# Cross-attention and feed-forward kernel: keys projected once instead of twice, their rotated half made by a DMA swap, context buffered twice

## The reference, cut to what matters

```python
# x: (4, 256, 128), ctx: (4, 512, 128); 16 heads of 64; B = 4 batches
lat = layer_norm(_layernorm(x), ln_lat_g, ln_lat_b)
ctx = layer_norm(context, ln_ctx_g, ln_ctx_b)
q = (lat @ Wq)                      # 256 x 1024 in each batch
k, v = split(ctx @ Wkv)             # 512 x 1024 each
# each head of 64 channels has two halves of 32
k = concat([k1 * cos - k2 * sin, k2 * cos + k1 * sin])
attn = softmax(clip(q k^T * 64 ** -0.5, -11, 11))
x = x + (attn v) @ Wo + bo
x = x + ffn(_layernorm(x))          # a second layer: products of 16 heads of 8, softmax,
                                    # two projections, 8 gated experts
```

## Time and profile before

| | |
|---|---|
| median of 3 runs | 391.61 us (391.37 to 391.96) |
| the profiled execution's own time | 388.52 us |
| its span, first to last instruction | 386.4 us |
| mean granted TensorE clock | 0.93 |
| TensorE matrix products busy | 321.9 us (83%) |
| VectorE busy | 269.6 us (70%) |
| GpSimd busy | 217.0 us (56%) |
| ScalarE busy | 155.5 us (40%) |

### The profile page before, as it was taken

One profiled execution on the slowest core, in us unless ns is written; L12 is line 12 of the kernel. 1 busy time (PEld: TensorE's weight loads), 2 busy tenths in 40 slices (PEclk: granted clock), 3 DMA queues, 4 the chain that ended last, 5 costly groups with the idle time before them and its releaser, 6 DMA issues.

```text
span 386.4 us, 6595 instructions
## 1 busy us (share of the span) xinstructions
PE 321.9 (83%) x2566; PEld 215.9 (56%) x2566; DVE 269.6 (70%) x459; ACT 155.5 (40%) x282; POOL 217.0 (56%) x200
## 2 busy tenths in 40 slices
PE   6699999999999989789999999599998986630444
PEld 6476666667776656457766566377665545310131
DVE  4886426337754799777585999774549879599844
ACT  3464544555324546215345556343444540100500
POOL 4767344355544483929346677973445876546070
PEclk9999999999999999969999999999999999755656
DMA  8730000000000000000000000000000000000000
GB/s 248 181 53 2 27 2 1 2 2 3 0 2 2 1 2 0 3 0 2 2 0 2 1 2 2 1 15 2 1 2 0 2 3 14 0 0 0 0 0 27
DMA packets 10157, 5.82 MB, mean 15 GB/s; under 512 B 2768, under 2 KB 9744, under 8 KB 10128
## 3 DMA queue, kind: packets, MB, share of 16 engines
q1 hardware_dynamic: 9072, 5.29, 5.3%
q10 hardware_dynamic: 1056, 0.13, 0.2%
HBM read 4.89 MB, written 0.52 MB: 14 GB/s over the span
## 4 chain that ended last, share of the span: by engine, by line
PE 53%; DVE 23%; POOL 10%; issue 6%; ACT 5%; DMA 2%; SPq 1%; DVEq 0%; POOLq 0%; ACTq 0%
PE sc L493 11%; PE pv L507 11%; PE sums L523 5%; POOL prod L823 5%; PE pj_k L434 5%; DVE prod L815 4%; PE pj_k L436 4%; PE pj_k L435 4%; DVE att L1003 4%; ACT e L688 3%; DVE o L1020 3%; PE side L580 3%; DMA prod<-in_L_xattn_Wq_dram 2%; DVE prod L823 2%; POOL wvS L1212 1%
## 5 line engine op out<-in xcount | busy, mean ns | idle before, releaser
L688 ACT ACTIVATE e<-sc 128x1024 f32<-128x1024 f32 x64 | 65.7, 1026 | 100.9 <-PE sc L493 100.9
L1225 POOL TENSOR_SCALAR e<-e 128x1024 f32<-128x1024 f32 x64 | 71.6, 1119 | 34.7 <-ACT e L688 30.9
L1218 POOL TENSOR_TENSOR krot<-kcos,ksin 128x512 f32<-128x512 f32 x32 | 41.7, 1304 | 69.7 <-DVE ksin L903 69.7
L493 PE MATMUL sc<-qs,ks 64*128 64x256 f32 x768 | 62.5, 295 | 6.3 <-ACT e L688 5.7
L493 PEld LDWEIGHTS sc<-qs,ks 64*128 64x128 f32 x768 | 49.4, 185 | 28.5 <-issue 16.6
L507 PE MATMUL pv<-e,v 128*64 128x256 f32 x512 | 64.0, 393 | 0.0
L507 PEld LDWEIGHTS pv<-e,v 128*64 128x64 f32 x512 | 34.5, 139 | 24.2 <-issue 9.3
L903 DVE TENSOR_TENSOR kcos<-pj_k,cosT 128x512 f32<-128x512 f32 x32 | 22.0, 688 | 30.2 <-PE pj_k L436 29.8
L523 PE MATMUL sums<-e,sum_rows 128*32 128x256 f32 x512 | 30.9, 382 | 5.3 <-POOL e L1225 5.3
L840 DVE TENSOR_TENSOR ks<-krot,ks 128x512 fp32r<-128x512 f32 x32 | 34.0, 1063 | 0.0
L823 POOL TENSOR_TENSOR prod<-att,kv 128x1024 f32<-128x1024 f32 x8 | 27.7, 3474 | 8.9 <-ACT att L779 8.6
(11 more groups left out here) (215 smaller groups left out, 596.3 us busy)
## 6 DMA issues: line engine op xcount, KB each, us to landing
ctx_in<-in_ctx_dram SPq DMA_DIRECT2D x4, 256.0 KB, 5.0
prod<-in_L_xattn_Wkv_dram SPq DMA_DIRECT2D x2, 512.0 KB, 6.0
x_in<-in_x_dram SPq DMA_DIRECT2D x1, 512.0 KB, 5.8
prod<-in_L_xattn_Wq_dram SPq DMA_DIRECT2D x1, 512.0 KB, 6.6
wo<-in_L_xattn_Wo_dram SPq DMA_DIRECT2D x1, 512.0 KB, 8.4
fwe<-in_L_ffn_We_dram SPq DMA_DIRECT2D x1, 512.0 KB, 4.3
out_dram<-x_in SPq DMA_DIRECT2D x4, 128.0 KB, 1.8
fbup_r<-in_L_ffn_bup_dram SPq DMA_DIRECT2D x1, 128.0 KB, 6.5
```

The costliest lines, as they stand in the source:

```text
L493: last = nc.tensor.matmul(sc[:, h, c * NT:(c + 1) * NT], ks[rows, j % 3, k_part, chunk], qs[rows, j % 2, q_part, :], start=(k_part + q_par ...
L688: nc.scalar.activation(e[:, j % 3, :, 2 * half:2 * half + 2, :].rearrange("p h c n -> p h (c n)"), sc[:, :, :], ACT.Exp, scale=SCALE).then ...
L1218: nc.gpsimd.tensor_tensor(krot[:, j % 2, :], kcos[:, j % 2, :], ksin[:, j % 2, :], ALU.add)\
L1225: nc.gpsimd.tensor_scalar(a, a, EXP_HIGH, EXP_LOW, ALU.min, ALU.max).then_inc(s_clip, 1)
```

## The change

Keys are projected with `wkA` alone, one slot earlier (`KEYS_AHEAD = 3`), and both products read that one bank: `ksin` first, then `kcos`. `ksin` then has its halves unexchanged; SyncE moves them with four DMAs of 32 partitions x 512 elements (64 KB each) into the new tile `kswap`, and `rotate`, still two slots ahead, adds `kcos` and `kswap`. The signs of the sine table are exchanged. `wkB` and its four copies go. The banks `pj_k` are handed out in the order of the projections, keys and values together, and a projection waits for the reader of the one before the last. `ctxT` has two buffers; `ctx_T` moves from (4, "c") to (3, "b") and `split_ctxT` from slot 8b+5 to slot 8b+4. In SyncE's queue the bias rows and contexts 2 and 3 are put between the swaps.

```diff
+KEYS_AHEAD = 3
-PREP_STEPS = {(4, "c"): "ctx_T", (6, "a"): "lat_T"}
+PREP_STEPS = {(3, "b"): "ctx_T", (6, "a"): "lat_T"}
...
+def projections():
+    units = []
+    for slot in range(-KEYS_AHEAD, LAST_SLOT):
+        if slot + KEYS_AHEAD < NPAIR:
+            units.append(("keys", slot + KEYS_AHEAD))
+        for n in value_units(slot):
+            if not value_units_at_first(n):
+                units.append(("values", n))
+    return units
+PROJECTIONS = projections()
+PLACE = {unit: i for i, unit in enumerate(PROJECTIONS)}
...
-        ctxT = sb("ctxT", [128, 2, NS], fp32r)
+        ctxT = sb("ctxT", [128, 2, 2, NS], fp32r)
+        kswap = sb("kswap", [128, 2, NS])
...
+        def key_bank(j):
+            return pj_k[PLACE["keys", j] % 2]
...
+            def swap_halves(j):
+                sp.wait_ge(s_kmul, 2 * j + 1)
+                if j >= 2:
+                    sp.wait_ge(s_krot, j - 1)
+                for r in range(4):
+                    to, at = HALF * r, HALF * (r ^ 1)
+                    sp.dma_start(kswap[to:to + HALF, j % 2, :], ksin[at:at + HALF, j % 2, :]).then_inc(s_kswap[j % 2], 16)
...
+            for j in range(NPAIR):
+                if j in (2, PAIRS):
+                    load_ctx(2 + j // PAIRS)
+                swap_halves(j)
+                for dst, src in later[j - 2:j - 1] if j >= 2 else ():
+                    sp.dma_start(dst, src).then_inc(ld["bias"], 16)
...
+            def bank_free(kind, n):
+                if PLACE[kind, n] < 2:
+                    return
+                kind, n = PROJECTIONS[PLACE[kind, n] - 2]
+                if kind == "keys":
+                    pe.wait_ge(s_kmul, 2 * n + 2)
+                else:
+                    pe.wait_ge(s_v, n + 1)
...
-                split3(pj_k[0][:, :], wkA[:, 0, cols], wkA[:, 1, cols], ctxT[:, 0, :], ctxT[:, 1, :]).then_inc(s_kproj, 1)
-                if j == 0:
-                    pe.wait_ge(s_wk, 2)
-                split3(pj_k[1][:, :], wkB[:, 0, cols], wkB[:, 1, cols], ctxT[:, 0, :], ctxT[:, 1, :]).then_inc(s_kproj, 1)
+                bank_free("keys", j)
+                split3(key_bank(j)[:, :], wkA[:, 0, cols], wkA[:, 1, cols], ctxT[:, b % 2, 0, :],
+                       ctxT[:, b % 2, 1, :]).then_inc(s_kproj, 1)
...
                 if j >= 2:
                     dve.wait_ge(s_krot, j - 1)
-                for i, (dst, bank, trig) in enumerate(((kcos, pj_k[0], cosT), (ksin, pj_k[1], sinT))):
-                    dve.wait_ge(s_kproj, 2 * j + i + 1)
-                    nc.vector.tensor_tensor(dst[:, j % 2, :], bank[:, :], trig[:, :], ALU.mult).then_inc(s_kmul, 1)
+                dve.wait_ge(s_kproj, j + 1)
+                for dst, trig in ((ksin, sinT), (kcos, cosT)):
+                    nc.vector.tensor_tensor(dst[:, j % 2, :], key_bank(j)[:, :], trig[:, :], ALU.mult).then_inc(s_kmul, 1)
...
-            for s in range(2):
-                src = f(wkA[:, s, :]).rearrange("k (h t i) -> k h t i", t=2, i=HALF)
-                dst = wkB[:, s, :].rearrange("k (h t i) -> k h t i", t=2, i=HALF)
-                for t in range(2):
-                    last = nc.vector.tensor_copy(dst[:, :, t, :], src[:, :, 1 - t, :])
-            last.then_inc(s_wk, 1)
...
-                if slot + KV_AHEAD < NPAIR:
-                    key_products(slot + KV_AHEAD)
-                if more and p == 5:
+                if slot + KEYS_AHEAD < NPAIR:
+                    key_products(slot + KEYS_AHEAD)
+                if more and p == 4:
                     split_ctxT(b + 1)
...
                 pool.wait_ge(s_kmul, 2 * j + 2)
+                pool.wait_ge(s_kswap[j % 2], 64 * (j // 2 + 1))
...
-                nc.gpsimd.tensor_tensor(krot[:, j % 2, :], kcos[:, j % 2, :], ksin[:, j % 2, :], ALU.add)\
+                nc.gpsimd.tensor_tensor(krot[:, j % 2, :], kcos[:, j % 2, :], kswap[:, j % 2, :], ALU.add)\
```

More of the change, by code:

```diff
@@ L174, in value_units, with value_units_at_first @@
     return []
-def value_units_before(slot):
-    return sum(len(value_units(s)) for s in range(-KV_AHEAD, slot))
+def value_units_at_first(n):
+    return n < 4
+def projections():
+    units = []
+    for slot in range(-KEYS_AHEAD, LAST_SLOT):
+        if slot + KEYS_AHEAD < NPAIR:
[6 more added lines that the diff above has]
+PLACE = {unit: i for i, unit in enumerate(PROJECTIONS)}
 def xattn_ffn(nc, x, ctx, cos, sin, ln_lat_g, ln_lat_b, ln_ctx_g, ln_ctx_b, Wq, Wkv, Wo, bo,
@@ L323, in xattn_ffn @@
         s_kmul = sem("s_kmul")
+        s_kswap = [sem(f"s_kswap{i}") for i in range(2)]
         s_krot = sem("s_krot")
@@ L464, in queries, with values @@
                 split3(pj_q[:, 0:NT], wqS[:, 0, cols], wqS[:, 1, cols], latT[:, 0, :], latT[:, 1, :]).then_inc(s_qproj, 1)
-            def values(n, slot):
+            def values(n):
                 b, unit = divmod(n, 8)
@@ L626, in _ @@
                 side_product(name, b)
-            for slot in range(-KV_AHEAD, LAST_SLOT):
-                if slot + KV_AHEAD < NPAIR:
-                    keys(slot + KV_AHEAD)
+            for slot in range(-KEYS_AHEAD, LAST_SLOT):
+                if slot + KEYS_AHEAD < NPAIR:
+                    keys(slot + KEYS_AHEAD)
                 if 0 <= slot < NPAIR:
@@ L639, in _ @@
                 for n in value_units(slot):
-                    values(n, slot)
+                    values(n)
                 side_at(slot, "b")
@@ L1275, in second_layer @@
                             sum_experts(b, t)
-            for slot in range(-KV_AHEAD, LAST_SLOT):
+            for slot in range(-KEYS_AHEAD, LAST_SLOT):
                 b, p = divmod(slot, PAIRS)
-                if slot + KV_AHEAD < NPAIR:
+                if 0 <= slot + KV_AHEAD < NPAIR:
                     rotate(slot + KV_AHEAD)
```

49 lines of the change are left out of this document (20 added, 29 removed).

## The result

The changed kernel takes 378.83 us (median of 4 runs, 378.15 to 379.52), the kernel before beside it 391.75 us (391.37 to 391.96): a ratio of 0.967 [0.965, 0.969], 12.9 us less. The forecast was 372.0 us. The profiled execution took 379.06 us with a span of 376.6 us; that of before had 386.4 us of span.

A forecast was written before the change was run, and what follows sets the result against it. Bound alternately by TensorE and VectorE stretches, then a dependent tail; 1.4 + 0.4 - 8.4 + 0.8 - 8.2 - 5.6 - 3.1 + 3.1 = -19.6 us, so 391.6 - 19.6 = 372.0 us. Range 366 to 381 us.

The forecast's parts named there:

- The removed projection: TensorE stretches: three products fewer, 0.70 us a pair, -8.4 us from 23 to 127.5 us and -5.6 us in later slots.
- The VectorE stretches: From VectorE's input to o_T, batches 0 and 1: 4.1 us less in each, -8.2 us.
- the wait of 2.03 us: VectorE's wait for GpSimd's weighted products ahead of reduce_1; forecast to close, counted as 2.0 us a stretch.
- the split's 2.1 us: The context's split moves from slot 13 to the start of slot 12, hidden in VectorE's idle time: 2.1 us a stretch.
- The second rival: GpSimd or another order keeps the ends: stretches give only the split's 2.1 us, last pairs 1.3 us; 377.8 us, chance 0.25.
- the base: Profiled execution before took 388.5 us, the runs' median 3.1 us more; the forecast subtracted 19.6 us from 391.6 us.
- The last pairs: After VectorE's input at 289.14 us: slot 29's key products move to slot 28, sums come earlier, -3.1 us.
- The bound that I named for "VectorE alone", 1.3 us: Last pairs: the other bound of the gain, 1.3 us by VectorE alone, beside the 3.1 us taken.
- The start: First scores at 24.4 us instead of 23.05 us, as the first swap has no slot in hand: +1.4 us.
- The swap elsewhere: Steady state: each swap has a whole slot of 7 to 9 us, so it costs nothing.
- The second clock fall: Around o_T of batch 1: a gap of about 4.3 us brings TensorE's clock to half rate, +3.1 us.

The follow-up runs named there:

- Run 8: Against the changed kernel, the rotates of pairs 15 to 17 and 23 to 25 add only 8 of 512 columns: 375.63 us, ratio 0.964.
- run 3: Against the changed kernel, GpSimd's rotate of each pair also waits for VectorE's products of the next pair: 378.07 us, ratio 0.971.
- run 2: Against the changed kernel, the swap DMAs are taken out and rotate adds ksin as it stands: 373.01 us, ratio 0.956.
- run 4: Against the kernel before, only two ctxT buffers, with its transposes one slot earlier and its split in slot 8b+4: 389.39 us, ratio 0.997.
- run 9: Against the changed kernel, 22 small identity products on TensorE ahead of o_T of batches 0 and 1: 375.16 us, ratio 0.961.

## Why the prediction was right or wrong

The direction and the range held (378.8 in 366 to 381); the size did not: -12.9 us measured against -19.6, and only -9.5 us by the profiled executions.

**The removed projection: right.** 0.70 us a pair where TensorE is the bound; 0.64 by the slots, 0.62 to 0.75 by the run that puts it back. The stretch from 166 to 209 us gave 2.56 us for a forecast of 2.4.

**The VectorE stretches, -8.2 us: this is the step that failed.** "So the wait of 2.03 us closes and VectorE alone ends the stretch" was true, and so was the split's 2.1 us; the timeline of after has neither. What was wrong was to keep VectorE's own durations as they were. I had moved GpSimd's instructions earlier without asking what VectorE does at that time. They then lay beside instructions of VectorE that read two inputs from SBUF, and the 4.1 us gained in each stretch came back as 4.1 and 4.5 us of longer instructions; with some shorter ones beside them, net 0.65 and 1.21 us. Run 8 shows the mechanism and 1.7 us of it in each stretch; that the other 2.4 us of the first are GpSimd's products over the two key rests is read from the rows, and agrees with run 3, where the second rest is back at 0.68 us with GpSimd's product behind it. It was not tried alone. The second rival had it, with the row of 4.48 us as its reason, and gave 377.8 us, the nearest of my numbers, in part by luck: it left the stretches 4.2 us where they gave 1.9, and the base, below, made up for it. It got 0.25; that row should have had more weight, because the forecast moved exactly the instructions that it speaks of.

**The last pairs, -3.1 us: too large for the same reason.** From kv at slot 28 to the sums of slot 29 the change saves 1.5 us: kv comes 8.1 us earlier and the sums, at 292.87 us against 302.45, 9.6 us earlier. The timeline of after, VectorE, then GpSimd:

```profile
281.85 5.66 DVE L855 TENSOR_TENSOR prod<-q,kv 128x1024 f32<-128x1024 f32 x2
289.00 2.36 DVE L880 TENSOR_TENSOR ks<-krot,ks 128x512 fp32r<-128x512 f32 x1
...
284.15 2.28 POOL L1253 TENSOR_TENSOR krot<-kcos,kswap 128x512 f32<-128x512 f32 x1
```

The same 5.66 and 2.36 us again. The bound that I named for "VectorE alone", 1.3 us, was the better one.

**The start, +1.4 us: mis-sized.** The first scores came 2.68 us later. ksin was 0.8 us later than I worked out, four issues took 0.62 us each instead of 0.48, and the key's rest 1.51 us instead of 1.1 (as in the same place before, at 21.12 us; 1.1 us is its mean over the kernel); the landing was 2.0 us, close to the 2.2 taken. The range of +0.9 to +5.7 us held it. Missing from the sum was the clock: TensorE stood for 4.34 us and the scores of pair 0 ran at half rate, 2 x 0.67 us more.

**The swap elsewhere: right**, hidden at no cost (run 2), and SyncE's issues are no bound: 4 x 0.62 us in a slot of 7.8 (slots 1 to 11 take 78.5 us).

**The second clock fall: right in kind, somewhat too dear.** It came, and costs 2.1 to 2.5 us, not 3.1. The Trainium skill, "TensorE: Matmul & The Clock Gate", section "Why this matters for your kernels", has the rule that I had weighed, that idle gaps between bursts of products send the clock down. The gaps of the change agree with it (4.34, 5.53 and 4.65 us, a fall behind each); the gap of 2.93 us ahead of the second o_T of before, with no fall, is the exception.

**The base.** By the profiled executions the kernel gained 9.5 us, by the medians 12.9. The profile of before stood 3.1 us under its median, that of after does not. Over 54 other executions of the kernel before, the span goes with the mean granted clock: 387.4 us on average for the five at 0.930 or more (as in the profile), 388.8 us for the seventeen at 0.921, 390.3 us for the four at 0.917 and 0.918. I take it that in most executions the second o_T met a slow clock that the profiled one escaped, so that the fall which I charged to the change was partly there already. The trace of run 4, whose second o_T has nearly the same gap as before, shows such a fall. PE in its timeline:

```profile
247.20 0.41 PE L530 MATMUL side<-ident,o 128*128 128x128 f32 x2 [2.95 <-DVE o L1023]
247.54 2.78 PE L507 MATMUL pv<-e,v 128*64 128x256 f32 x16
```

In before the second row took 1.95 us, and from this o_T to the next kv it is 42.04 us against 40.45. So such a gap can go either way. That it did so in most executions of before is argued, not shown: only one of them has a trace.

**Open:** why the split alone gave only 0.6 us in the second stretch, and why the 22 products of run 9 gave 2.5 us by the ratios and 4.0 by the profiles.

## What to carry to other kernels

Before moving a GpSimd instruction to an earlier time, look at what VectorE does at that time. Where VectorE's instruction reads two inputs from SBUF, as its products and the key's rest here, and GpSimd's reads SBUF, as its products, adds and clips do, the one that comes second waits for the other to end, and an idle time that it seemed to remove may have been what kept the two apart. Shortening one engine's work widens another's gap, so read the granted clock behind every gap: here gaps of 4.34, 5.53 and 4.65 us each brought a fall, worth 2.1 to 2.5 us at o_T. Filling the gaps ahead of o_T paid with products about as long as the gap (5.18 us) and cost time with longer ones (9.20 us).

## What the runs showed of the hardware that I had not expected

- VectorE and GpSimd wait for whole instructions of each other: the add of 8 columns took 1.18 us beside VectorE's products and 0.20 alone, the add of 512 columns 2.26 and 1.28, the same 0.98 us of waiting.
- A copy from SBUF to SBUF of 64 KB landed in 2.0 us, and its issue took 0.62 us on SyncE's queue (5.00 us for 8), more than the 0.43 us of a small load.
- TensorE's clock fell after gaps of 4.34, 5.53 and 4.65 us, and stayed up when the same time was filled with products of no use; at the two o_T that gained 2.5 us in the whole. After gaps of 2.93 and 2.95 us ahead of the second o_T it stayed up in the kernel before and fell in run 4.
- A product of two 128x128 blocks in float32 takes two passes of 0.115 us (80 in 9.20 us).
